# Expert attention in a six-layer decoder kernel: routing both halves at once, half the weights split a layer early, gates spread by DMA, rows turned once, and unread products at four layer ends

## The reference

```python
logits = normalize(flat, -1) @ normalize(sim_matrix, 0) - sigmoid(gates)
gated = relu(logits)
# experts with a positive logit; where none, the top two
# gate = softmax(gated) over the selected of 16 experts
```

## Time and profile before

| | |
|---|---|
| median of 3 runs | 697.14 us (696.58 to 698.10) |
| the profiled execution | 697.67 us, of it the span 695.4 us |
| PE busy, share of the span | 492.4 us, 71% |
| DVE | 449.6 us, 65% |
| ACT, POOL | 257.1 us, 37%; 211.2 us, 30% |
| mean granted clock of PE | 0.835 |
| first to last instruction of layer 3 | 246.7 to 365.6 us |

### The profile page before, as it was taken

One profiled execution on the slowest core, in us unless ns is written; L12 is line 12 of the kernel. 1 busy time (PEld: TensorE's weight loads), 2 busy tenths in 40 slices (PEclk: granted clock), 3 DMA queues, 4 the chain that ended last, 5 costly groups with the idle time before them and its releaser, 6 DMA issues. The chain is left out here.

```text
span 695.4 us, 11548 instructions
## 1 busy us (share of the span) xinstructions
PE 492.4 (71%) x4041; PEld 361.4 (52%) x4041; DVE 449.6 (65%) x1433; ACT 257.1 (37%) x621; POOL 211.2 (30%) x246
## 2 busy tenths in 40 slices
PE   4598436383588556898865777868679778899960
PEld 2265323363577356677653455757347645455540
DVE  4579888989474787754365499897378546133225
ACT  4599601110003433453103545653245422143331
POOL 2223001445430072533001332240164126234440
PEclk9789757587899857998985778899679969999995
DMA  8100015100000040000000000000454001501012
GB/s 286 28 3 2 1 39 204 32 2 1 0 1 1 0 119 1 1 1 1 1 0 1 0 1 2 2 1 1 179 238 111 22 0 45 145 23 32 32 35 90
DMA packets 26115, 29.28 MB, mean 42 GB/s; under 512 B 5112, under 2 KB 21224, under 8 KB 25545
## 3 DMA queue, kind: packets, MB, share of 16 engines
q1 hardware_dynamic: 24124, 25.08, 11.2%
q0 software_dynamic: 1504, 3.15, 1.4%
q10 hardware_dynamic: 432, 0.33, 0.2%
HBM read 22.40 MB, written 6.15 MB: 41 GB/s over the span
## 5 line engine op out<-in xcount | busy, mean ns | idle before, releaser
L3310 DVE TENSOR_TENSOR em_inner<-banks,em_soft 128x256 f32<-128x256 f32 x31 | 13.2, 425 | 52.4 <-ACT em_soft L3146 52.4
L3194 POOL DMA_INDIRECT em_results<-em_y_slot,slot_rows x31 | 29.8, 960 | 49.6 <-DVE em_y_slot L3318 48.7
L198 ACT ACTIVATE norm_log<-norm_var 128x4 f32<-128x4 f32 x20 | 4.1, 205 | 92.8 <-DVE norm_var L181 92.7
L3084 PE MATMUL banks<-em_up,em_slotT 128*128 x62 | 34.9, 645 | 0.0
L1769 POOL TENSOR_TENSOR ea_scaled_rows<-ea_scaled_rows 128x768 f32<-128x768 f32 (+1 forms) x16 | 22.6, 1414 | 38.1 <-ACT ea_scaled_rows L1672 37.5
L2351 POOL TENSOR_TENSOR ga_to_end<-ga_cum 128x512 f32<-128x512 f32 x8 | 12.4, 1546 | 68.2 <-DVE ga_cum L2407 68.1
L38 PE MATMUL banks<-ea_w_high,ea_x_high 128*128 128x384 f32 x64 | 26.3, 411 | 9.6 <-DVE ea_acc L1858 9.5
L1672 ACT ACTIVATE ea_scaled_rows<-banks,ea_gate 128x192 f32<-128x192 f32 x64 | 23.3, 420 | 24.9 <-PE banks L38 22.8
L1172 POOL TENSOR_TENSOR xa_prob<-xa_score,xa_top 128x308 f32<-128x308 f32 x8 | 5.6, 705 | 76.7 <-DVE xa_left L1264 76.7
L3146 ACT ACTIVATE em_soft<-banks 128x256 f32<-128x256 f32 x31 | 11.9, 385 | 42.8 <-PE banks L3084 42.8
L552 POOL TENSOR_TENSOR lin_q_strip<-lin_qT,lin_strip_head 128x512 f32<-128x512 f32 x8 | 13.9, 1743 | 42.8 <-PE banks L434 28.6
(11 more groups left out here) (505 smaller groups left out, 1535.2 us busy)
## 6 DMA issues: line engine op xcount, KB each, us to landing
em_up<-in_em_up SPq DMA_DIRECT2D x3, 1536.0 KB, 12.2
em_down<-in_em_down SPq DMA_DIRECT2D x3, 768.0 KB, 13.8
em_slots<-slot_rows SPq DMA_DIRECT2D x1, 2108.0 KB, 9.8
w_qkv<-in_w_qkv SPq DMA_DIRECT2D x1, 1536.0 KB, 6.4
slot_rows<-em_slots SPq DMA_DIRECT2D x1, 1360.0 KB, 8.3
cos_lag<-in_cos_lag SPq DMA_DIRECT2D x1, 1024.0 KB, 5.6
sin_lag<-in_sin_lag SPq DMA_DIRECT2D x1, 1024.0 KB, 7.9
cos_half<-in_cos_half SPq DMA_DIRECT2D x1, 1024.0 KB, 10.1
```

Of the source, the lines that this page charges most:

```text
L3084: pe.matmul(s.ps[:, :], slotT[:, n], up_all[:, bass.ds(e, 1), :], start=False, stop=True, skip_group_check=True).then_inc(s.filled, 1)
L3194: pool.indirect_dma_start(core.results[:, :], bass.IndirectOffsetOnAxis(ap=slot_rows[:, s, P:P + 1].bitcast(U32), axis=0), y_slot[:, s % N ...
L3310: dve.tensor_tensor(inner[:, n % NW], s.ps[:, HE:2 * HE], soft[:, n % NW], ALU.mult).then_inc(inner_ready, 1)
```

## The change

1. Routing of both halves at once, all of it ahead of the first tile: cubes of 128 elements a partition in place of 64.
2. Weights of experts 8 to 15 are rounded and lowered in layer 2 (ACT and POOL), with two small bfloat16 constants. Those of experts 0 to 7 are rounded on ACT in four pieces of two experts and lowered on DVE, one piece early and three behind the gates. x is rounded on ACT and lowered on DVE out of PSUM; POOL has no part in it.
3. Sizes of x come from the variance and root of the preceding norm (`Norm.last`).
4. Gates are turned in tiles 0 and 1 as float32, 16 rows; SP stores them to DRAM (64 KB) and reads them back in four broadcasts of 1 MB, one a half and a parity of experts, each to 64 partitions. The spreading products go, `weigh` reads SBUF, and all eight products of a half may be ahead.
5. POOL adds `acc` into the sum, so PE turns the rows of a tile by one transpose.
6. The tail is in a new order, `finish(0)` after all weighings.
7. `KeepBusy`: products of 512 columns that nothing reads, 8, 5, 3 and 4 of them behind PE's last work in layers 2 to 5.

Removed bodies (`compare`, `choose`, `normalise`, `split_gates`, `spread_pair`, POOL's splits) are to be seen above and left out here. In layer 2 `up` takes the place of the tile `far`.

```diff
+    def __call__(self, pe, x, count):
+        s = self.slot
+        s.claim(pe)
+        for n in range(count):
+            ins = pe.matmul(s.ps[:, :], self.core.tiles["ident"][:, :], x[:, 0:HT], start=True, stop=True)
+            if n in (0, count - 1):
+                ins.then_inc(s.drained if n else s.filled, 1)
...
+    def last(self):
+
+        k = (self.on_dve - 1) % 2
+        return self.mean_var[:, k, :, 1], self.root[:, k]
...
+                core.wait_loaded(act, "ea")
+                act.copy(core.ident16[:, :], ident[:, :]).then_inc(core.rounded, 1)
+                act.copy(core.bias16[:, :], t["causal_bias"][:, :]).then_inc(core.rounded, 1)
+                for n in range(3):
+                    act.copy(columns(core.w_high, n), columns(t["w_qkv"], 3 + n)).then_inc(core.rounded, 1)
...
+                add_bias(0)
+                pool.wait_ge(y_ready, 2 * B)
+                for n in range(3):
+                    pool.wait_ge(core.rounded, n + 3)
+                    low_part(pool, columns(core.w_low, n), columns(t["w_qkv"], 3 + n), columns(core.w_high, n)
+                             ).then_inc(core.w_split, 1)
+                add_bias(1)
...
+                    if b < B - 1:
+                        var, root = core.norm.last()
+                        step(dve.tensor_tensor(core.size[:, hb], var, root, ALU.mult))
+                        step.mark(dve.scalar_tensor_tensor(core.size[:, hb], core.size[:, hb], float(C), root, ALU.mult,
+                                                           ALU.mult))
...
+                for b in range(B):
+                    ring[f"gateT{b}"].taken(sp)
+                sp.dma_start(core.gates[:, :, :], gateT[:, :, :]).then_inc(gates_spread, 16)
+                sp.wait_ge(gates_spread, 16)
+                for b in range(B):
+                    for n in range(2):
+                        one = core.gates[n:NE:2, b, :]
+                        sp.dma_start(wide[HD * n:HD * n + HD, :, b, :], one.partition_broadcast(HD)
+                                     ).then_inc(gates_spread, 16)
...
-                logits(1)
+                s = ring["logit"]
+                s.claim(pe)
+                for g in range(NT):
+                    if g % HT == 0:
+                        pe.wait_ge(x_moved, g // HT + 1)
+                    ins = pe.matmul(s.ps[:, g * NE:(g + 1) * NE], xT[:, g], t["sim"][:, :], start=True, stop=True,
+                                    skip_group_check=True)
+                ins.then_inc(s.filled, 1)
+                pe.wait_ge(core.rounded, 5 + 4)
...
+                    n, e = divmod(2 * j, NE // 2)
+                    if g == 0:
+                        if n == 0:
+                            pe.wait_ge(lowered, j + 1)
+                        else:
+                            pe.wait_ge(core.w_split, 3)
...
                     pe.wait_ge(summed, g + 1)
-                    pe.matmul(s.ps[:, 0:P], acc[:, g % 2, 0:2 * HD], ident[:, :], start=True, stop=False)
-                    pe.matmul(s.ps[:, 0:P], scaled_rows[:, g % 2, 0, 0:2 * HD], ident[:, :], start=False,
-                              stop=True).then_inc(s.filled, 1)
+                    pe.transpose(s.ps[:, 0:P], qkv_rows[:, g % 2, 0:2 * HD], ident[:, :]).then_inc(s.filled, 1)
...
+                    if g < B:
+                        turn_gates(g)
...
+                        pe.wait_ge(weighed, n + 1)
...
                 mix(0, (0, 1))
                 turn_prob(NT - 2)
+                turn_rows(NT - 1)
                 mix(0, (2,))
-                turn_rows(NT - 1)
-                mix(0, (3,))
                 attend(NT - 2)
                 score(NT - 1)
-                mix(0, (4, 5))
+                mix(0, (3, 4))
                 turn_prob(NT - 1)
-                mix(0, (6, 7))
+                mix(0, (5, 6, 7))
                 attend(NT - 1)
-                for j in range(LEAD):
-                    spread_pair(1, j)
                 ring["out1"].claim(pe)
                 mix(1, range(PAIRS))
+                keep_busy(pe, x, 5)
...
+                    act.copy(xT[:, half(b)], s.ps[:, :]).then_inc(x_moved, 1)
+
+                def round_x(b):
+                    act.copy(x_high[:, half(b)], ring[f"xT{b}"].ps[:, :]).then_inc(x_moved, 1)
+
+                def round_weights(n):
+                    act.copy(w_high[0][:, 2 * n:2 * n + 2], t["w_qkv"][:, 2 * n:2 * n + 2]).then_inc(core.rounded, 1)
...
                 round_weights(0)
                 move_x(0)
                 act.wait_ge(squares, 3)
                 step(act.activation(size_log[:, :], size[:, :], ACT.Ln, scale=float(2 ** 40)))
                 act.activation(unit[:, :], size_log[:, :], ACT.Exp, scale=-0.5).then_inc(exps, 1)
+                move_x(1)
+                round_x(0)
+                for n in range(1, 4):
                     round_weights(n)
+                round_x(1)
+                act.wait_ge(gating, 1)
+                act.activation(rest[:, :], rest[:, :], ACT.Exp).then_inc(exps, 1)
+                act.wait_ge(gating, 2)
...
+                    if 1 <= g <= B:
+                        s = ring[f"gateT{g - 1}"]
+                        s.ready(act)
+                        act.copy(gateT[:, g - 1], s.ps[0:NE, :]).then_inc(s.drained, 1)
                     scale_pair(g, 1)
...
-                    for n in (4, 2):
+                    for n in (4, 2, 1):
                         step(pool.tensor_tensor(scaled_rows[:, k, 0:n], scaled_rows[:, k, 0:n],
                                                 scaled_rows[:, k, n:2 * n], ALU.add))
-                    pool.tensor_tensor(scaled_rows[:, k, 0], scaled_rows[:, k, 0], scaled_rows[:, k, 1],
-                                       ALU.add).then_inc(summed, 1)
+                    ring[f"unit{g}_6"].taken(pool)
+                    if g >= 2:
+                        ring[f"qkT{g - 2}"].ready(pool)
+                        pool.wait_ge(v_ready, g - 1)
+                    pool.tensor_tensor(qkv_rows[:, k], scaled_rows[:, k, 0], acc[:, k], ALU.add).then_inc(summed, 1)
...
+                last = half(B - 1)
+                var, root = core.norm.last()
+                step(dve.tensor_tensor(size[:, last], var, root, ALU.mult))
+                step(dve.scalar_tensor_tensor(size[:, last], size[:, last], float(C), root, ALU.mult, ALU.mult))
...
+                def lower_x(b):
+                    s = ring[f"xT{b}"]
+                    dve.wait_ge(x_moved, 3 + b)
+                    dve.tensor_tensor(x_low[:, half(b)], s.ps[:, :].rearrange("p (i t) -> p i t", i=HT),
+                                      x_high[:, half(b)].bitcast(F32), ALU.subtract).then_inc(s.drained, 1)
+
+                def lower_weights(n):
+                    dve.wait_ge(core.rounded, 5 + n + 1)
+                    low_part(dve, w_low[0][:, 2 * n:2 * n + 2], t["w_qkv"][:, 2 * n:2 * n + 2],
+                             w_high[0][:, 2 * n:2 * n + 2]).then_inc(lowered, 1)
+
+                lower_weights(0)
...
+                lower_x(0)
...
+                dve.tensor_tensor(lg, s.ps[:, 0:NT * NE].rearrange("p (i e) -> p i e", i=NT), scale[:, :],
+                                  ALU.mult).then_inc(s.drained, 1)
+                s.taken(dve)
+                step(dve.tensor_tensor(lg, lg, spread(sigma[:, :], 1, cube), ALU.subtract))
+                for g in range(NT):
+                    step.mark(dve.max(best[:, g], logit[:, g]))
+                step.mark(dve.tensor_scalar(ch, lg, 0.0, None, ALU.is_gt))
+                step.mark(dve.tensor_scalar(gt, lg, 0.0, None, ALU.max))
+                step.wait()
+                step(dve.tensor_scalar(most[:, :], best[:, :, 0], 0.0, None, ALU.max))
+                dve.tensor_tensor(gt, gt, spread(most[:, :], 2, cube), ALU.subtract).then_inc(gating, 1)
+                step.mark(dve.tensor_scalar(few[:, :], best[:, :, 0], 0.0, None, ALU.is_le))
+                step(dve.memset(best[:, :, 2:8], SELECTED))
+                for g in range(NT):
+                    step.mark(dve.match_replace(second[:, g], best[:, g], logit[:, g], SELECTED))
+                step.wait()
+                step(dve.scalar_tensor_tensor(se, se, SELECTED, spread(few[:, :], 2, cube), ALU.is_equal, ALU.mult))
+                step(dve.tensor_tensor(ch, ch, se, ALU.max))
+                dve.wait_ge(exps, 3)
+                step(dve.tensor_tensor(gt, gt, ch, ALU.mult))
+                step(dve.tensor_reduce(most[:, :], gt, AX.X, ALU.add))
+                step(dve.reciprocal(most[:, :], most[:, :]))
+                dve.tensor_tensor(gate[:, :], gt, spread(most[:, :], 2, cube), ALU.mult).then_inc(gating, 1)
+                for n in range(1, 4):
+                    lower_weights(n)
+                dve.wait_ge(gating, 2)
...
+                    dve.tensor_copy(v2[:, g], spread(qkv_rows[:, g % 2, 2 * HD:], 1, [P, 2, HD])).then_inc(v_ready, 1)
...
```

(19 more changed lines are left out.)

212 lines of the change are left out of this document (44 added, 168 removed).

## The result

The changed kernel takes 671.99 us (median of 4 runs, 671.23 to 674.13) where the kernel before takes 697.02 (696.58 to 698.1): a ratio of 0.9644, 95% interval 0.9618 to 0.9669, 25.0 us faster. The forecast was 22.3 faster, 674.8 us. The profiled execution took 671.23 us, 669.4 of it span, at a mean granted clock of 0.851 (0.835 before).

The account below looks back on a forecast made before the run. PE was taken to bound layer 3's middle, with waits at both ends. Layer 3 gives -17.8 us (-10.4 - 7.7 + 0.3), spare products -4.5, together -22.3: 674.8 us on the median of 697.14, range 667 to 685.

Parts of the forecast that it names:

- Start of layer 3: Layer 3 up to its first addition: gates 4.4 us earlier, at 257.9, and first addition at 259.5 against 262.5, -3.0.
- a silent POOL: Start of layer 3: eight DVE operations take 1.8 us in all instead of 8.45 without POOL's work beside them, -6.7.
- First tile: Layer 3's first tile: ends no earlier than the -3.0 at the first addition allows, -2.9 where the second tile starts.
- PE by then has one pair done, not four: First tile of layer 3: PE has fewer pairs ready at the first addition, so -3.0 there becomes -2.9.
- Second tile and projections: Layer 3: stalls of 2.73 and 2.87 us go; -6.0 by the second tile's sum, -4.4 more by the projections' end, -10.4.
- POOL's wait: Second tile of layer 3: PE waits 1.0 us for POOL's longer sum, and 0.4 in the next tile.
- Broadcast: Store and four 1 MB transfers in layer 3: 13 to 26 us, landed between 286 and 300, first use about 314, cost 0.
- Tail: Layer 3 after the projections: PE busy 25.9 plus waits 5.6, together 31.5 us instead of 39.2, -7.7.
- The waits: Layer 3's tail: PE waits for transposed probabilities, weighings and handovers, followed through the new order, 5.6 us in all.
- Sixteen spreads go: Layer 3's tail: PE loses sixteen spreading products, 0.33 us each clear of their neighbours, -5.3.
- Spare products: Ends of layers 2 to 5: hidden in PE's idle, they keep the clock for layers 3 to 6, -4.5 in all.
- layer 3's 0.4: Start of layer 3: spare products at layer 2's end make its first products 0.4 us faster.

Follow-up runs that it names:

- e12: Changed kernel with all six POOL subtractions, three big and three small, put back at the start of layer 3: ratio 0.9636 to the kernel before.
- e8: Changed kernel plus spare products in two PE waits of layer 3, three behind the first pair and two ahead of the first mixing: 666.45 us, ratio 0.9524.
- e9: Changed kernel with gates made in two halves again, the second half's routing among the additions of tiles 1 and 2: 679.71 us, ratio 0.9613.
- e1: Changed kernel without any of its spare products at the ends of layers 2 to 5: 687.36 us, ratio 0.9717.
- e6: Changed kernel with POOL's three big subtractions moved from layer 2 to the start of layer 3: ratio 0.9645.
- e7: Changed kernel with an unread 512-column bfloat16 product ahead of each of the tail's 16 mixings: 675.46 us, ratio 0.9652.

## Why the prediction was right, point by point

**Start of layer 3.** Gates 4.43 earlier against 4.4; first addition 3.34 against 3.0. The sum held. Its largest term, 6.7 us for a silent POOL, can't be had by itself: with six of POOL's subtractions back, 6.7 us of its work, the gates are 1.7 later (e12), since DVE waits for PE in the new order and has slack there. POOL's casts and low parts of x, the rest of its 12.21 us, weren't put back.

**First tile.** Predicted no shorter and no longer than before, -3.0 becoming -2.9; it took 6.61 us instead of 5.68, and the second tile started 2.4 earlier. The step that failed is "PE by then has one pair done, not four": it counted the pairs, and not that they would run at half clock (0.65 on average from 256.90 to 263.50). e8 shows it, 4.30 us with the clock up.

**Second tile and projections.** The second tile is 2.6 us shorter (predicted 3.1) with POOL's wait at 1.24 (predicted 1.0), and e9 gives 2.4 for the halves alone; from the third tile to the last addition -4.1 against -4.4. At the end of the projections 9.2 are won, not 10.4.

**Broadcast.** Cost 0, landed by 297.6 where 286 to 300 was said, hidden by 15 us. The 4.2 MB took at most 25 us, inside the bounds of 13 and 26. The Trainium skill's figure for 64 partitions ("SBUF — State Buffer", section "Door 1: The DMA port swizzle") gave an estimate of 21 us, and the trace is near it.

**Tail.** 29.2 us from the end of the last addition (310.04) to that of the last mixing (339.27), not 31.5. The waits were as followed (29.2 - 23.1 = 6.1, predicted 5.6); PE's busy time is 23.1, not 25.9. The mis-sized term is "Sixteen spreads go (0.33 clear of their neighbours, -5.3": at 0.48 each it is -7.7. That same speed made `finish(1)` late: it began 1.7 us after the last mixing, since `finish(0)` holds DVE 4.9 us. From the last mixing to layer 4 it is 7.12 us instead of 5.51, +1.6 where +0.3 was allowed. Together -9.2 - 9.8 + 1.6 = -17.4 for the layer against -17.8. That the two agree so well is partly luck: the projections gave 1.2 less and the end 1.3 less, the tail 2.1 more, and the clock alone moves the tail by as much.

**Spare products.** Predicted 4.5, measured 5.1 and 6.9 by two routes with wide intervals. By layers, layer 3's 0.4 didn't show (e1's gates are as early), and the idle left ahead of layer 4 was 2.98 us, not 1.2, since `finish(1)` was late. The clock's fall was delayed rather than prevented: in the changed kernel it came 0.2 us ahead of layer 3's start, 0.4 after layer 4's, 1.9 after layer 5's and 2.4 after layer 6's.

**What came above the forecast.** 2.7 us in the medians, 4.1 in the profiles (26.4 against 22.3). Of those, 2.3 lie in layer 2, where the same instructions take 143.8 to 146.1 from one execution to the next. Layer 4 gave 3.2 where 0.6 was predicted; without spare products it takes 125.32 (e1), so they aren't the cause of most of it. In the profile before, the clock is at 0.50 for the first 21 us of layer 4; in the changed kernel it rises after some 14, and in e1, without them, after 13. Whether 128.0 is typical of the kernel before stays open: it has one profile.

## What to carry to other kernels

When an engine falls idle just ahead of a critical stretch, price the stretch at the clock it will have then, not at the one of the rows: five unread products in two waits of layer 3 won about 4 us of it. Price a removed instruction by the period of the pattern with and without it, not by its own duration (0.48, not 0.33). And work of POOL on SBUF cost DVE up to one stall for each of its instructions here, so it belongs beside DVE's waits. Before a difference of a microsecond or two is given to a change, compare the clock's low stretches in both profiles.

## What the runs showed of the hardware

- The same instructions, from layer 3's first mixing to those of the second half, took 16.9 to 19.1 us by the length of the stretch at 0.50 (3.4 to 10.2 us).
- A DVE operation of 0.11 us that started beside a POOL subtraction took 1.15 (e6); so did one on 24 elements with a single SBUF operand (0.18 to 1.00); those that came next passed at 0.15 to 0.17.
- From 244.7 to 251.3 in the changed kernel PE made transposes, sixteen-column products and one pair at a clock of 0.50, then waited 4.93 us, and the clock rose at 261.5. With three 512-column products in that wait (e8) it rose at 256.8.
- A 512-column bfloat16 product between groups of eight float32 records adds 0.48 us to each period (1.41 against 0.92, e7), 0.16 beyond its own 0.33.
- A store of 64 KB took 1.9 us, and four broadcasts of it to 64 partitions each, 1 MB a piece, at most 25 us together.
